# Turning the third batch's context behind the first residuals, and issuing the first x2's transposes ahead of the second half of w2

## The chip, the cores and the metric

The kernel runs on one core of one Trainium2 chip. The metric is the device time of one execution in microseconds (us), as the median of the runs. TensorE (PE) multiplies, VectorE (DVE), ScalarE (ACT) and GpSimd (POOL) do the rest, and SyncE (SP) issues nearly all DMAs from one queue of its own, in program order.

## The reference, cut to what matters

Four batches of 512 rows of width 512, with a context of 512 rows of width 256 each, go through cross attention and a feed-forward layer whose weights are quantised to -1, 0 and 1 inside the kernel.

```python
def _bit_quant(w):
    scale = jnp.maximum(jnp.mean(jnp.abs(w)), EPS)
    w_ternary = jnp.clip(jnp.round(w / scale), -1.0, 1.0)
    return w + jax.lax.stop_gradient(w_ternary - w)

# attention, teacher_logits = layernorm(x), teacher_features = ctx
query = einsum('bnc,dc->bnd', ctx, Wq) + bq
key = einsum('bnc,dc->bnd', ctx, Wk) + bk
attention = softmax(einsum('bnd,bmd->bnm', query, key), axis=-1)
x = x + einsum('bln,bmn->blm', layernorm(x), attention)

# feed-forward, w1 is (2048, 512), w2 is (512, 2048)
h = gelu(einsum('bsd,fd->bsf', layernorm(x), _bit_quant(w1)) + b1)
x = x + einsum('bsf,df->bsd', h, _bit_quant(w2)) + b2
```

The scale of a weight matrix is a mean over the whole matrix: nothing of w2 can be rounded before the last quarter of w2 has landed and been summed.

## The kernel before, in words

Each engine has a program written out by hand, and semaphores tie them together; an engine does its instructions in exactly the order written. Batches are numbered 0 to 3, and each has four row tiles of 128.

SP loads ctx 0, x 0, the biases, ctx 1, x 1, then w1 (two halves, each four DMAs of 512 KB, L253), ctx 2 (`load_ctx(2)`, L245), then both halves of w2 (`load_w(1, 0)` and `load_w(1, 1)`, L253 too). Then it issues `turn_x2(0)` (L257): two DMA transposes of the layer-normed x2 of batch 0, one for its high fp16 part and one for its low part, 512 KB each, from a staging area (`gT_lo` for batch 0) into `x2T`. SP waits for `x2_hi_done` ahead of the first and for `x2_lo_done` ahead of the second. Behind them stand b2, x 2, ctx 3 and x 3.

DVE turns a context by a 32x32 block transpose (`turn_ctx`, L735), which the projections (PE, L409) need. After the attention product of batch 0 (PE, L460) it adds the residual (`residual`, L794), takes the moments (`moments2`, L800, and `aggregate2`, L807), and POOL makes x2n of them (`layernorm2`, L325 to L350). ACT casts x2n to its high part (`high_x2`, L648) and DVE subtracts for the low part (`low_x2`, L755). DVE also copies the low part of the turned probabilities of batch 1 (`low_turned_probs(1)`, L741).

The scale of w1 and of w2 is found like this: ACT sums absolute values of eight chunks (`sum_abs`, L672; chunks 0 to 3 are the first half of the matrix in SBUF, 4 to 7 the second, and it waits for each half's semaphore), DVE adds the eight sums (`abs_rows`, L811), PE sums over the partitions (`total`, L441), and DVE makes the scale and its inverse (`quantiser_scale`, L815 and L818). POOL then rounds the matrix in eight chunks of two instructions (`round_weights`, L372 and L375), and DVE clamps and turns each chunk (`quantise`, L849 and L856).

PE's order around the change is: attend(0), the turned probabilities of batch 1 (L435), project(2) (L409), attend(1) with total(W1) inside it, the first quarter of the hidden layer of batch 0 (`hidden(0, 0)`, L475, 32 matmuls), total(W2), the other three quarters (96 matmuls), and the output product of batch 0 (`output(0, t)`, L492), which needs the turned chunks of w2 one after another. The hidden layer goes through four PSUM banks: ACT applies the gelu (L680), writes the high part (L685), DVE writes the low part (`low_gelus`, L862), and only then may PE write the bank again.

ACT's order is: `sum_abs(0, (6, 7))`, `copy_qk(2)` (L622, which copies the projections of batch 2 out of PSUM), `high_x2(0)`, `sum_abs(1, range(8))`, then the gelus of batch 0. DVE's order there is `low_x2(0)`, `residual(1, 0)`, `quantiser_scale(W1)`, the other residuals of batch 1 among quantise(0, 0..3), `abs_rows(W2)`, `low_gelus(0, (0, 1))`, `quantise(0, 4)`, `low_gelus(0, (2, 3))`, `quantiser_scale(W2)`.

Of the kernel before, what the change touches and what calls it, by code (L numbers as in the profile page):

```python
# [25 lines left out]
def xattn_ffn(nc, x, ctx_in, Wq, bq, Wk, bk, w1, b1, w2, b2, out):  # L26
# [20 lines left out]
    with ExitStack() as stack:  # L47
# [64 lines left out]
        def x2_stage(b):  # L112
            return lo_stage[:, 0] if b == 0 else w1_stage[:, b % 2]

        def xn_stage(b):
            return w2_stage[:, 0]

        def probs_stage(b):
            return w2_stage[:, 1]
# [14 lines left out]
        def xnT(b):  # L134
            return turned_half(b, 0)

        def probsT(b):
            return turned_half(b, 1)
# [88 lines left out]
        def e_rows(tile):  # L227
            return tile.rearrange("p (s i) -> p s i", s=2)
# [10 lines left out]
        @block.sync  # L239
        def _(sp):  # L240
            def load_ctx(b):
                if b:
                    sp.wait_ge(ctxT_ready, b)
                for q in range(Q):
                    sp.dma_start(ctx_sb[q * R:(q + 1) * R], ctx_view[b, q]).then_inc(ctx_here, 16)  # L245

            def load_x(b):
                sp.dma_start(x_sb[:, b], x_tiles[b]).then_inc(x_here[b], 16)

            def load_w(m, h):  # L250
                n = raws[m].shape[1] // 2
                for q in range(Q):
                    sp.dma_start(raws[m][q * R:(q + 1) * R, h * n:(h + 1) * n, :],  # L253
                                 w_views[m][q, :, h * n:(h + 1) * n, :]).then_inc(w_here[m][h], 16)

            def turn(dst, stage, v, here):
                sp.dma_start_transpose(dst[:, v].rearrange("p j (t k) -> p (j t) k", t=NT), stage[:, v]).then_inc(here, 16)  # L257

            def turn_x2(b):
                if b >= 2:  # L260
                    sp.wait_ge(hidden_ready, NF * (b - 1))
                sp.wait_ge(x2_hi_done, NT * (b + 1))
                turn(x2T[:, b % 2], x2_stage(b), 0, x2T_here[b])
                sp.wait_ge(x2_lo_done, NT * (b + 1))
                turn(x2T[:, b % 2], x2_stage(b), 1, x2T_here[b])

            def turn_xn(b):
                if b > EARLY:
                    sp.wait_ge(attn_ready, NT * b)
                sp.wait_ge(xn_hi_done, NT * (b - EARLY + 1))  # L270
                turn(xnT(b), xn_stage(b), 0, xnT_here[b - EARLY])
                sp.wait_ge(xn_lo_done, NT * (b - EARLY + 1))
                turn(xnT(b), xn_stage(b), 1, xnT_here[b - EARLY])

            def turn_probs(b):
                sp.wait_ge(probs_hi_done, NT * (b - EARLY + 1))
                turn(probsT(b), probs_stage(b), 0, probsT_here[b - EARLY])
                sp.wait_ge(probs_lo_done, NT * (b - EARLY + 1))
                turn(probsT(b), probs_stage(b), 1, probsT_here[b - EARLY])

            def store(b, tiles=range(NT)):
                for t in tiles:
                    sp.wait_ge(y_done, NT * b + t + 1)
                    sp.dma_start(out_tiles[b, :, t], x_sb[:, b, t]).then_inc(out_done, 16)

            load_ctx(0)
            load_x(0)
            sp.dma_start(bqk[:, 0:1], bq.rearrange("(p a) -> p a", a=1)).then_inc(bqk_here, 16)
            sp.dma_start(bqk[:, 1:2], bk.rearrange("(p a) -> p a", a=1)).then_inc(bqk_here, 16)
            load_ctx(1)  # L290
            load_x(1)
            load_w(0, 0)
            load_w(0, 1)
            load_ctx(2)
            load_w(1, 0)
            load_w(1, 1)
            turn_x2(0)
            sp.dma_start(b2_sb[:], b2.rearrange("(a d) -> a d", a=1).to_broadcast([P, D])).then_inc(b2_here, 16)
            load_x(2)
            load_ctx(3)  # L300
            load_x(3)
            turn_x2(1)
            turn_xn(2)
            turn_probs(2)
            store(0)
            turn_x2(2)
            turn_xn(3)
            turn_probs(3)
            store(1)
            turn_x2(3)  # L310
            store(2)
            store(LAST, range(NT - 1))
            for n, columns in enumerate(HALVES):
                sp.wait_ge(y_done, NT * B + n)
                sp.dma_start(e_rows(out_tiles[LAST, :, NT - 1])[:, :, HALF_ROWS[n]],
                             e_rows(x_sb[:, LAST, NT - 1])[:, :, HALF_ROWS[n]]).then_inc(out_done, 16)
            sp.wait_ge(out_done, 16 * (B * NT + 1))
# [412 lines left out]
        def _(dve):  # L730
            def turn_ctx(b):
                dve.wait_ge(ctx_here, 16 * Q * (b + 1))
                if b:
                    dve.wait_ge(qk_ready, 2 * b)
                nc.vector.transpose(ctxT[:].rearrange("p k (tb r) -> p tb k r", r=R),  # L735
                                    ctx_sb[:].rearrange("p tb (c k) -> p tb k c", c=R)).then_inc(ctxT_ready, 1)

            def low_turned_probs(b, tiles=range(NT)):
                for j in tiles:
                    dve.wait_ge(probsT_hi_done, NT * b + j + 1)  # L740
                    nc.vector.tensor_tensor(probsT(b)[:, 1, j], ps_t[j][:], probsT(b)[:, 0, j],  # L741
                                            ALU.subtract).then_inc(bank_read[j], 1)

            def low_turned_xn(b):
                for j in range(ND):
                    dve.wait_ge(xnT_hi_done, ND * b + j + 1)
                    nc.vector.tensor_tensor(xnT(b)[:, 1, j], ps_t[j][:], xnT(b)[:, 0, j],
                                            ALU.subtract).then_inc(bank_read[j], 1)
# [49 lines left out]
            def moments2(b, t):  # L798
                dve.wait_ge(x2_done, NT * b + t + 1)
                nc.vector.bn_stats(stats2[:, t], x_sb[:, b, t]).then_inc(stats2_done, 1)  # L800

            def aggregate2(b):
                if b:
                    dve.wait_ge(rstd2_done, b)
                for t in range(NT):
                    dve.wait_ge(stats2_done, NT * b + t + 1)
                    nc.vector.bn_aggr(mv2[:, t], stats2[:, t]).then_inc(mv2_done, 1)  # L807

            def abs_rows(m):
                dve.wait_ge(abs_done, NCH * m)  # L810
                nc.vector.tensor_reduce(abs_row[:, m:m + 1], abs_sum[:, m - 1], AX.X, ALU.add).then_inc(abs_row_done, 1)  # L811
# [87 lines left out]
            for t in range(1, NT):  # L899
                inverse(1, t)  # L900
            low_turned_xn(1)
            turn_ctx(2)
            for t in range(NT):
                residual(0, t)
                moments2(0, t)
            aggregate2(0)
            low_turned_probs(1)
            abs_rows(W1)
            low_x2(0)
# [137 lines left out]
```

## Time and profile before

| | us |
|---|---|
| median of 3 runs | 326.37 |
| lowest and highest | 325.68, 327.33 |
| the profiled execution: its own time | 325.16 |
| the profiled execution: its span in the trace | 323.6 |
| PE busy | 306.2 (95% of the span) |
| DVE, ACT, POOL busy | 167.8, 146.9, 114.4 |

The profile is of one execution, and starts of instructions are counted in us from its span's start. An entry such as "[7.05 <-DMA x2T<-gT_lo]" behind an instruction says how long its engine was idle ahead of it and what ended that. A row of the timeline can merge several instructions of one kind ("x32"). The mean granted clock of TensorE is 0.989 of full speed.

### The profile page before, as it was taken

What the parts mean: (1) busy time and instruction counts of PE and PEld (TensorE: products, weight loads), DVE (VectorE), ACT (ScalarE), POOL (GpSimd) and SP (SyncE); (2) the same over time, 40 slices, a digit from 0 to 9 for tenths busy, and PEclk for the clock granted to TensorE, in tenths of its full rate; (3) what the DMA queues carried; (4) which work ended last, traced back from release to release, by engine and by line L of the source; (5) the groups of instructions that cost most, each with busy time, mean ns of one, the idle gap of its engine ahead of it and who ended that gap; (6) DMA issues with size and microseconds to landing.
All of it is one profiled execution on the core that took longest, in us unless ns stands there. A gap on an engine that the chain in (4) does not pass through costs nothing.

```text
span 323.6 us, 3680 instructions
## 1 busy us (share of the span) xinstructions
PE 306.2 (95%) x1397; PEld 143.8 (44%) x1397; DVE 167.8 (52%) x295; ACT 146.9 (45%) x255; POOL 114.4 (35%) x124
## 2 busy tenths in 40 slices
PE   6989999199999799999999999999999999999995
PEld 3445454044444344444444444444444444444454
DVE  2896398847999587463533822533533103342101
ACT  2186977657750752564274350565260006772000
POOL 0355017998999976000280470000290000000000
PEclk9999999789999999999999999999999999999999
DMA  8999999992000497500003676000006210000011
GB/s 218 255 207 213 195 222 214 177 240 77 0 2 0 83 131 144 164 2 0 0 0 67 125 135 194 2 0 0 2 4 117 75 51 15 0 2 0 32 61 38
DMA packets 57857, 28.03 MB, mean 87 GB/s; under 512 B 42736, under 2 KB 51696, under 8 KB 57840
## 3 DMA queue, kind: packets, MB, share of 16 engines
q1 hardware_dynamic: 57472, 27.53, 40.4%
q10 hardware_dynamic: 368, 0.27, 0.4%
q8 instruction: 11, 0.18, 0.2%
q14 instruction: 6, 0.05, 0.1%
HBM read 15.21 MB, written 4.19 MB: 60 GB/s over the span
## 4 chain that ended last, share of the span: by engine, by line
PE 67%; POOL 11%; SPq 10%; DMA 5%; DVE 3%; ACT 1%; issue 1%; POOLq 0%
PE ps_t L475 28%; PE ps_e L492 28%; PE ps_e L460 6%; SPq L253 5%; DMA ctx_sb<-in_ctx 3%; POOL w_raw L372 3%; POOL w_raw L375 3%; SPq L245 3%; POOL x2n L350 2%; PE ps_e L499 2%; DMA x2T<-gT_lo 2%; PE ps_e L416 2%; SPq L257 2%; POOL x_sb L366 2%; PE ps_e L409 1%
## 5 line engine op out<-in xcount | busy, mean ns | idle before, releaser
L475 PE MATMUL ps_t<-x2T,w1T 128*128 128x512 f16 x512 | 113.7, 382 | 7.1 <-DMA x2T<-gT_lo 7.1
L492 PE MATMUL ps_e<-w_raw,gT_hi 128*128 128x512 f16 x240 | 91.0, 379 | 0.0
L492 PE MATMUL ps_e<-w_raw,gT_lo 128*128 128x512 f16 x240 | 91.0, 379 | 0.0
L680 ACT ACTIVATE ps_t<-ps_t,b_col 128x512 f32<-128x512 f32 x64 | 42.5, 665 | 94.8 <-PE ps_t L475 94.8
L475 PEld LDWEIGHTS ps_t<-x2T,w1T 128*128 128x128 f16 x512 | 50.4, 99 | 68.6 <-DMA x2T<-gT_lo 7.5
L862 DVE SCALAR_TENSOR_TENSOR gT_lo<-ps_t,h_scale,gT_hi 128x512 f16<-128x512 f32 x64 | 44.9, 743 | 64.8 <-ACT gT_hi L685 64.8
L685 ACT ACTIVATE gT_hi<-ps_t,h_scale 128x512 f16<-128x512 f32 x64 | 40.3, 685 | 0.0
L868 DVE SCALAR_TENSOR_TENSOR x_sb<-ps_e,h_unscale,x_sb 128x512 f32<-128x512 f32 x15 | 11.2, 747 | 55.2 <-PE ps_e L492 55.2
L325 POOL TENSOR_SCALAR var_eps<-mv 128x4 f32<-128x4 f32 x8 | 1.9, 240 | 98.7 <-DVE mv L807 86.1
L492 PEld LDWEIGHTS ps_e<-w_raw,gT_lo 128*128 128x128 f16 x240 | 23.5, 98 | 29.3 <-issue 1.7
L492 PEld LDWEIGHTS ps_e<-w_raw,gT_hi 128*128 128x128 f16 x240 | 23.5, 98 | 29.1 <-issue 1.2
L375 POOL TENSOR_SCALAR w_raw<-w_raw 128x1024 f16<-128x1024 f32 x16 | 21.8, 1363 | 1.4
L460 PE MATMUL ps_e<-w_raw 128*128 128x512 f16 x96 | 21.7, 379 | 0.0
L358 POOL TENSOR_SCALAR probs<-probs,row_inv 128x512 f32<-128x512 f32 x16 | 13.9, 885 | 21.3 <-DVE row_inv L780 21.3
L366 POOL TENSOR_TENSOR x_sb<-x_sb,b_sb 128x512 f32<-128x512 f32 x16 | 21.3, 1362 | 0.0
L372 POOL TENSOR_SCALAR w_raw<-w_raw,inv_scale 128x1024 f32<-128x1024 f32 x16 | 19.2, 1202 | 3.2 <-DVE inv_scale L818 3.2
L628 ACT ACTIVATE probs<-ps_e,row_max 128x512 f32<-128x512 f32 x16 | 10.9, 686 | 19.0 <-DVE row_max L775 18.9
L672 ACT ACTIVATE abs_out<-w_raw 128x1024 uint8<-128x1024 f32 x16 | 17.0, 1061 | 1.4 <-DMA w_raw<-in_L_ffn_w 1.0
L416 PE MATMUL ps_e<-qkT 128*128 128x512 f32 x32 | 14.9, 598 | 2.5 <-ACT probs L628 1.8
L409 PE MATMUL ps_e<-ctxT,WT 128*128 128x512 f32 x32 | 14.5, 595 | 1.4 <-DVE ctxT L735 1.4
L460 PEld LDWEIGHTS ps_e<-w_raw 128*128 128x128 f16 x96 | 9.4, 98 | 11.3
L350 POOL TENSOR_SCALAR x2n<-x_sb,neg_mean,rstd 128x512 f32<-128x512 f32 x16 | 14.0, 888 | 0.5
(82 smaller groups left out, 275.7 us busy)
## 6 DMA issues: line engine op xcount, KB each, us to landing
w_raw<-in_L_ffn_w SPq DMA_DIRECT2D x16, 512.0 KB, 10.4
x_sb<-in_x SPq DMA_DIRECT2D x4, 1024.0 KB, 6.8
out<-x_sb SPq DMA_DIRECT2D x15, 256.0 KB, 2.5
ctx_sb<-in_ctx SPq DMA_DIRECT2D x16, 128.0 KB, 5.1
b_sb<-in_L_ffn_b SPq DMA_DIRECT2D x1, 256.0 KB, 6.7
out<-x_sb SPq DMA_DIRECT2D x2, 128.0 KB, 2.2
x2n<-in_L_xattn_Wq ACTq DMA_DIRECT2D x1, 128.0 KB, 2.6
x2n<-in_L_xattn_Wk ACTq DMA_DIRECT2D x1, 128.0 KB, 3.3
```

What stands on the lines that cost most here:

```text
L350: nc.gpsimd.tensor_scalar(x2n[:, t].rearrange("p (j q c) -> p q j c", j=ND, q=Q), x_sb[:, b, t].rearrange("p (q j c) -> p q j c", q=Q, j=N ...
L366: nc.gpsimd.tensor_tensor(x_sb[:, b, t], x_sb[:, b, t], b2_sb[:], ALU.add).then_inc(b2_added, 1)
L372: nc.gpsimd.tensor_scalar(src, src, inv_scale[:, m:m + 1], ROUND, ALU.mult, ALU.add).then_inc(scaled, 1)
L375: nc.gpsimd.tensor_scalar(chunk_whole(m, c).rearrange("p n (i s) -> p n s i", s=2), src, -ROUND, 1.0, ALU.add, ALU.mult).then_inc(rounded, 1)
L409: mm = nc.tensor.matmul(ps_e[s][:], WT[:, s, k], ctxT[:, k], start=(k == 0), stop=(k == NC - 1))
L416: nc.tensor.matmul(attn_bank(b, t)[:], qkT[:, 0, t * P:(t + 1) * P], qkT[:, 1], start=True, stop=True).then_inc(scores_ready, 1)
L460: mm = nc.tensor.matmul(attn_bank(b, t)[:], xnT(b)[:, u, j, t * P:(t + 1) * P], probsT(b)[:, v, j], start=(n == 0 and j == 0), stop=(n == ...
L475: mm = nc.tensor.matmul(ps_t[t][:], w1T[:, k // 2, j, :, k % 2], x2T[:, b % 2, v, j], start=(v == 0 and j == 0), stop=(v == 1 and j == ND ...
L492: mm = nc.tensor.matmul(y_bank(t)[:], part[:, k, t * P:(t + 1) * P], w2T[:, k], start=(k == 0 and part is gT_hi), stop=(k == NF - 1 and pa ...
L680: nc.scalar.activation(ps_t[t][:], ps_t[t][:], ACT.Gelu, scale=1.0 / LN_SCALE, bias=b1_col[:, k:k + 1]).then_inc(gelu_done, 1)
L685: nc.scalar.activation(gT_hi[:, k], ps_t[t][:], ACT.Identity, scale=h_scale[:, 0:1]).then_inc(gT_hi_done, 1)
L862: nc.vector.scalar_tensor_tensor(out=gT_lo[:, k], in0=ps_t[t][:], scalar=h_scale[:, 0:1], in1=gT_hi[:, k], op0=ALU.mult, op1=ALU.subtract) ...
```

## The change

Two steps of two programs are written in another place; nothing is added or taken out. On SP, `turn_x2(0)` now stands between the two halves of w2. On DVE, `turn_ctx(2)` now stands behind the four residuals and the moments of batch 0, ahead of the low parts of the turned probabilities of batch 1.

```diff
             load_ctx(2)
             load_w(1, 0)
+            turn_x2(0)
             load_w(1, 1)
-            turn_x2(0)
             sp.dma_start(b2_sb[:], b2.rearrange("(a d) -> a d", a=1).to_broadcast([P, D])).then_inc(b2_here, 16)
...
             low_turned_xn(1)
-            turn_ctx(2)
             for t in range(NT):
                 residual(0, t)
                 moments2(0, t)
             aggregate2(0)
+            turn_ctx(2)
             low_turned_probs(1)
```

On SP the piece of the program between w1 and b2 reads as follows (L253 is a load of weights, L245 of ctx, L257 a transpose of x2's staging area, L298 b2):

```order
 L253 DMA w_raw<-in_L_ffn_w 32x32x128 x8
 L245 DMA ctx_sb<-in_ctx 32x16x64 x4
-L253 DMA w_raw<-in_L_ffn_w 32x8x512 x8
+L253 DMA w_raw<-in_L_ffn_w 32x8x512 x4
 L257 DMA_TRANSPOSE x2T<-gT_lo 128x16x128 x2
+L253 DMA w_raw<-in_L_ffn_w 32x8x512 x4
 L298 DMA b_sb<-in_L_ffn_b 128x512
 L248 DMA x_sb<-in_x 128x4x512
```

The last four loads of w2, and all behind them, now stand behind two instructions that wait for ACT and DVE.

On DVE, between the low parts of batch 1's turned xn (L747) and the first residual of batch 0 (L794), the context's turn is gone:

```order
 L747 TENSOR_TENSOR gT_hi<-ps_t2,gT_hi 128x512
 L747 TENSOR_TENSOR gT_hi<-ps_t3,gT_hi 128x512
-L735 STREAM_TRANSPOSE ctxT<-ctx_sb 128x16x2x32
 L794 SCALAR_TENSOR_TENSOR x_sb<-ps_e0,x_sb 128x512
 L800 BN_STATS stats2<-x_sb 128x6
```

The residuals of batch 0 no longer stand behind the wait for ctx 2. It comes back behind the eight instructions of residuals and moments and the aggregation, ahead of batch 1's turned probabilities (L741):

```order
 L800 BN_STATS stats2<-x_sb 128x6
 L807 BN_AGGR mv2<-stats2 128x2 x4
+L735 STREAM_TRANSPOSE ctxT<-ctx_sb 128x16x2x32
 L741 TENSOR_TENSOR gT_hi<-ps_t0,gT_hi 128x512
 L741 TENSOR_TENSOR gT_hi<-ps_t1,gT_hi 128x512
```

The projections of batch 2 (PE) and what copies them (ACT) wait for this instruction. PE, ACT and POOL keep their programs.

## Rows read from the trace of the kernel before

**Rows 1.** Waits of PE over the whole span: total us, times, longest

```profile
PE ps_t L475 <- DMA x2T<-gT_lo: 7.1, 1, 7.1
PE ps_e L416 <- ACT probs L628: 1.8, 1, 1.8
```

**Rows 2.** Chain that ended last, in order of time: start us, us, what

```profile
48.44 4.00 POOL x2n L350 x4
...
53.10 5.23 SPq L257
...
58.39 5.95 DMA x2T<-gT_lo
64.38 8.52 PE ps_t L475 x32
...
126.86 6.91 PE ps_t L475 x32
```

**Rows 3.** Timeline of DVE from 34 us: start us, us, instruction [idle before <-releaser]

```profile
39.82 1.25 DVE L735 STREAM_TRANSPOSE ctxT<-ctx_sb 128x1024 f32<-128x1024 f32 x1 [5.04 <-DMA ctx_sb<-in_ctx]
...
44.92 0.68 DVE L794 SCALAR_TENSOR_TENSOR x_sb<-ps_e,x_sb 128x512 f32<-128x512 f32 x1
...
49.89 3.92 DVE L755 TENSOR_TENSOR gT_lo<-x2n,gT_lo 128x512 f16<-128x512 f32 x4 [0.85 <-ACT gT_lo L648]
...
70.96 1.41 DVE L862 SCALAR_TENSOR_TENSOR gT_lo<-ps_t,h_scale,gT_hi 128x512 f16<-128x512 f32 x2 [3.92 <-ACT gT_hi L685]
```

**Rows 4.** Timeline of PE from 40 us

```profile
40.62 1.91 PE L435 MATMUL ps_t<-ident,probs 128*128 128x128 f32 x16
42.36 3.60 PE L409 MATMUL ps_e<-ctxT,WT 128*128 128x512 f32 x8
...
72.86 20.88 PE L475 MATMUL ps_t<-x2T,w1T 128*128 128x512 f16 x96
```

**Rows 5.** Timeline of ACT from 45 us

```profile
45.44 1.25 ACT L622 ACTIVATE qkT<-ps_e,bqk 128x512 f32<-128x512 f32 x2
...
58.64 1.06 ACT L672 ACTIVATE abs_out<-w_raw 128x1024 uint8<-128x1024 f32 x1 [0.97 <-DMA w_raw<-in_L_ffn_w]
...
63.15 0.19 ACT L672 ACTIVATION_READ_ACCUMULATOR abs_out<-w_raw 128x1 f32 x1
67.79 1.28 ACT L680 ACT_TABLE_LOAD   x1 [4.45 <-PE ps_t L475]
...
73.51 1.26 ACT L685 ACTIVATE gT_hi<-ps_t,h_scale 128x512 f16<-128x512 f32 x2
```

**Rows 6.** Timeline of SP's issues: start us, us on SP

```profile
37.56 0.45 SPq L253 DMA_DIRECT2D w_raw<-in_L_ffn_w  x1
...
108.88 1.89 SPq L257 DMA_TRANSPOSE x2T<-w_raw  x1
...
110.82 2.62 SPq L257 DMA_TRANSPOSE x2T<-w_raw  x1
```

**Rows 7.** DMA view, us from issue to landing: issue of 37.56, then of 110.82

```profile
w_raw<-in_L_ffn_w SPq DMA_DIRECT2D x1, 512.0 KB, 11.9
...
x2T<-w_raw SPq DMA_TRANSPOSE x1, 4.8
```

**Rows 8.** Windows: us, busy PE, PEld, DVE, ACT, POOL, PEclk, DMA share, GB/s

```profile
50.00:56.00 6.00, 6.00 (x29) 2.71 (x28) 5.60 (x10) 4.71 (x8) 3.58 (x4) 1.00 1.07 216
...
62.00:64.00 2.00, 0.00 (x0) 0.00 (x0) 1.93 (x4) 1.30 (x4) 1.91 (x3) 0.50 0.94 107
...
110.00:115.00 5.00, 3.91 (x14) 1.75 (x15) 2.77 (x5) 3.54 (x9) 4.89 (x6) 1.00 1.11 208
```

**Rows 9.** Timeline of POOL from 54 us

```profile
54.77 1.12 POOL L372 TENSOR_SCALAR w_raw<-w_raw,inv_scale 128x1024 f32<-128x1024 f32 x1 [2.34 <-DVE inv_scale L818]
...
73.77 1.34 POOL L375 TENSOR_SCALAR w_raw<-w_raw 128x1024 f16<-128x1024 f32 x1
75.99 1.25 POOL L372 TENSOR_SCALAR w_raw<-w_raw,inv_scale 128x1024 f32<-128x1024 f32 x1 [0.87 <-DVE inv_scale L818]
```

## The prediction, made before the changed kernel had run

> **What bounds the kernel now.** I read the waits of PE first: in the whole span PE waits long for one thing only, 7.1 us for the transposes of x2, and the next wait is 1.8 us for an exponential of batch 2 [rows 1]. PE is busy for 95% of the span (the table above), so only what lies before that second wait can move the end. The chain, read next, goes through exactly this place: POOL makes x2n until 52.44, ACT's last cast ends about 53.1, SP spends 5.23 us on the first transpose (its ring still holds w2), the second is issued at 58.39 and lands at 64.34, and PE starts the hidden layer at 64.38 [rows 2]. So the change attacks the longest wait of the kernel. But the chain does not stay with PE. POOL starts rounding w1 at 54.77, ends at 75.11, starts w2 at 75.99, for which it waited 0.87 us on the inverse scale [rows 9], and from there POOL, not PE, carries the chain through eight chunks of w2, b2, the second layernorm of batch 1 and the exponentials, to PE's wait of 1.8 us. In this stretch the end is therefore set by **when POOL may start w2**, and PE has 1.8 us of air. The question is what the change does to that start.
>
> **The context behind the residuals.** DVE sat idle for 5.04 us for ctx 2 while the attention products of batch 0 were coming out [rows 3]. PE ends the last of them at about 40.8 (it starts the next work at 40.62, with some overlap) [rows 4]. The first three residuals are then done, and the fourth starts at about 40.85 in place of 44.92 [rows 3], so POOL's x2n moves about 4.1 us forward, from 48.44 to 44.3, and ends at 48.3 [rows 2]. What it costs: the turn of the context, 1.25 us [rows 3], now starts when the aggregation is over, at 42.5, and ends at 43.7. PE's projection starts there and not at 42.36, takes its 3.60 us and ends at 47.3 [rows 4]. ACT copies the second of its two results only then, 0.6 us each [rows 5], to 47.9, and this stands ahead of the casts of x2n. Four casts at 0.65 us (the last ended 53.1, and four of them back to back take 2.6) end at 50.5: **2.6 us sooner, not 4.1**. DVE's four subtractions took 3.92 us [rows 3], start about 48.6 and end at 52.5, 1.3 us sooner than 53.8. DVE's scale of w1 comes right behind, so POOL starts w1 at about 53.5 instead of 54.77 and would end at 73.9 instead of 75.1 [rows 9].
>
> **The transposes ahead of half of w2.** The first half of w2 was issued by 37.56 and landed 11.9 us later, at 49.5 [rows 6, 7]. The ring is then empty. The nearest rows for a transpose pair from an empty ring are those of batch 1: issued at 108.88 and 110.82, SP held for 1.89 and 2.62 us, the second landing 4.8 us after its issue [rows 6, 7]. From 50.5 this gives the first issue at 50.5, the second at 52.5, landing at 57.3: 7 us sooner than 64.34. PE is in attend(1) until about 58.6 (57.3, which is 64.38 less its wait of 7.1, plus the 1.35 us by which the projection is late), so hidden(0, 0) starts there, 5.7 us sooner, with no idle time ahead of it, at the full clock, in 6.91 us, and ends at 65.5 [rows 2].
>
> **What stands behind the moved transposes.** SP issues the last four loads of w2 after them, at 52.5 + 2.6 = 55.1, in place of right behind the issue of 37.56. Before, DMA was full all the time: 216 GB/s and a share of 1.07 between 50 and 56 [rows 8], and the second half landed at 58.6, 9.1 us behind the first (ACT's wait ended by it) [rows 5, 7]. Now DMA lies idle from 49.5 to about 51.6, and then moves the 1 MB of the transposes first. The half is 2.10 MB: 9.7 us at 216 GB/s, 9.1 us by the landings; I take 9.4. It starts when the transposes are through: 57.3 + 9.4 = **66.7, which is 8 us later** than 58.6.
>
> Who waits for it: ACT. Its chunks 4 to 7 took from 58.64 to 63.34, 4.7 us [rows 5], and stand ahead of every gelu. They end at 71.4. Before, ACT was through at 63.34 and idle for 4.45 us until PE's first tiles; the table load started at 67.79 [rows 5]. Now it starts at 71.4, 3.6 us later, though PE has had the four tiles ready since 65.5. From here the steps are counted in rows of before: DVE's first low part started 3.17 us after the table load (70.96 against 67.79) [rows 3, 5], so with 1.41 us for the first two DVE is busy until 4.6. The second pair's high parts can start 4.7 us after the table load: 1.28 for it, 2.3 for the first pair's gelus and high parts, 1.16 for two gelus. The high parts' start to POOL's start on w2 was 73.51 to 75.99, 2.5 us [rows 5, 9]; about 0.25 us is added by quantise(0, 4), which stands between the pairs on DVE. Together 7.45 us: POOL starts w2 at 71.4 + 7.45 = 78.9, against 75.99 [rows 9]: **2.9 us later**. The 2.2 us that POOL's earlier end of w1 might have given become idle time of POOL.
>
> PE's own way: bank 0 is read 3.9 us after the table load, so hidden(0, 1) starts at 71.4 + 3.9 = 75.3, against 72.86 [rows 4], 2.4 us later. PE is idle for 9.8 us ahead of it. In its idle time of before the granted clock fell to 0.50, which is 1.2 GHz [rows 8], and the first 32 matmuls took 8.52 us where 32 take 6.91 at full clock [rows 2]: 1.6 us that are now paid behind this stall. PE would be 4.0 us late, and with its 1.8 us of air [rows 1] 2.2 us late. POOL is the later one. The loss is POOL's 2.9 us, since from PE's wait of 1.8 us on nothing is idle that could take it back.
>
> **The sum.** Against the profiled execution's own time, 325.16 + 2.9 = 328.1 (its span 323.6 becomes 326.5). That execution lay 1.2 us under the median of the runs, so against the median: 326.4 + 2.9 = 329.3.
>
> **A rule weighed.** Two transposes of 512 KB each kept DMA at a share of 1.11 and 208 GB/s between 110 and 115 [rows 8], 5 us for 1 MB. The Trainium skill, in "DMA: Bandwidth & Descriptors", section "Latency and other measured facts", gives 261 GB/s for such a transpose; an estimate by that page is 4.0 us for both, the half of w2 would land 1.0 us sooner, and the loss would be 1.9 us. The trace doesn't agree with it.
>
> **The rivals.** (a) *The half of w2 and the transposes overlap.* If it flows from its issue on, it lands at 55.1 + 9.4 = 64.5 and the loss is 0.7 us: 327.1, which is no change. Against it: batch 1's pair alone kept the DMA engines' share at 1.11 [rows 8], so it leaves no room for that. (b) *Faster.* The mechanism is that w2's scale is ready when POOL ends w1 at 73.9. Then POOL's chain is 1.2 us early and only that is gained, since POOL's rounding is the bound: about 325.2. It decides at a landing of 61.6 (73.9 less 7.45, less 4.7), 6.5 us after the issue at 55.1, with 1 MB of transposes ahead; the rows give more than 11. A change that gains more than 1.2 us I see no mechanism for. (c) *SP is held as it was before.* It spent 5.23 us on the first transpose in place of 1.89 [rows 2, 6]. If that was the transpose's own cost and not the full ring, the second is issued at 55.7 and everything behind it is 3.2 us later: a loss of 6.1, 332.5. (d) *PE becomes the bound* by a low clock that lasts. If the 32 matmuls of hidden(0, 1) ran wholly at 1.2 GHz, they cost 6.9 us and not 1.6: 2.4 + 6.9 - 1.8 = 7.5 us, 333.9. Rows of before show it for a part of the 32 only. In mild form (the half of w2 at 68, the same clock) it stays under POOL. (e) *The transposes start no sooner*, because ACT's casts don't move: then the pair is issued from 53.1 and the half of w2 is 2.6 us later still, 331.9. Against it: nothing else stands ahead of the casts.
>
> The Trainium skill, "TensorE: Matmul & The Clock Gate", section "HAM oscillation — how this bites in real kernels", says that a wait for DMA between bursts of matmuls puts the array back to its low clock each time. The trace agrees in the one wait it has (0.50 in rows 8); by this rule the new wait costs PE its start-up again, which is (d) in its mild form, and a kernel is not helped by trading one such wait for a longer one.
>
> **How the numbers follow.** The forecast, 2 to 5.2 us lost, has 0.68; a loss under that but above 1.6 us 0.05; (a), with what else lies within 0.5%, 0.14; (b) 0.02; (c), (d) and (e) together 0.09; 0.02 is left for a gain without a mechanism that I see. The range 326.8 to 331.6 takes in (a), and at its upper end the half of w2 at 9.7 us with 2 us more for a ring that starts from empty; it leaves out (b), (c), (d) and (e). A measurement of this kernel can tell about 0.5% (1.6 us) from no change. Faster by more than that 0.02, within it 0.16 ((a) and (b)), slower 0.82.
>
> **What would show it.** In the profile of the changed kernel: DVE's four residuals run before ctx 2 is turned, with the turn at about 42.5; the casts of x2n end about 50.5; the transposes are issued at 50.5 and 52.5; PE's 7.1 us wait at L475 for DMA is gone, and in its place hidden(0, 1) waits about 9.8 us for DVE's low parts of the gelus; ACT waits some 11 us at L672 for DMA of w2, until 66.7; POOL starts w2 at 78.9 after some 5 us of idle time. The prediction is wrong if ACT's wait ends before 65, or if POOL starts w2 before 77.6, or if PE's later wait at L416 doesn't stay (at 0.7 to 1.8 us), which would make PE the bound.

## The result, and the profile after

The changed kernel is slower, and by more than the range allowed for: 332.26 us (331.51 to 333.2) against 326.02 us (325.44 to 327.33), a ratio of 1.0187 with a 95% interval of 1.014 to 1.0234. That is 6.2 us where 2.9 were forecast. The profiled execution took 331.51 us with a span of 329.9 us. Three of the experiments below have one execution far out (939, 481 and 977 us), which is left out of their ratios and of the times given for them.

The waits of PE over the span, to hold against [rows 1]:

```profile
PE ps_e L441 <- DVE abs_row L811: 9.2, 1, 9.2
PE ps_t L475 <- DVE gT_lo L862: 3.2, 1, 3.2
...
PE ps_t L475 <- DMA x2T<-gT_lo: 0.3, 1, 0.3
```

The wait of 7.1 us for the transposes is down to 0.3, as meant. In its place PE waits 9.2 us for the sum of w2's rows and 3.2 us for the first gelus' low parts. The wait of 1.8 us at L416 is gone.

The first part of the change did what was expected of it. DVE's timeline, answering [rows 3]:

```profile
41.34 0.69 DVE L794 SCALAR_TENSOR_TENSOR x_sb<-ps_e,x_sb 128x512 f32<-128x512 f32 x1 [1.17 <-PE ps_e L460]
...
42.95 1.21 DVE L735 STREAM_TRANSPOSE ctxT<-ctx_sb 128x1024 f32<-128x1024 f32 x1
...
49.19 2.50 DVE L755 TENSOR_TENSOR gT_lo<-x2n,gT_lo 128x512 f16<-128x512 f32 x4 [2.59 <-ACT gT_lo L648]
```

The last residual starts at 41.34 and not at 44.92, the context is turned right behind the moments, and the low parts take 2.50 us in place of 3.92 and end at 51.7. The issues of SP and, from the DMA view, the times to landing of the transposes issued at 50.73 and 52.75 and of w2's loads issued at 56.47 and 58.07, answering [rows 6, 7]:

```profile
50.73 5.69 SPq L257 DMA_TRANSPOSE x2T<-gT_lo  x2
56.47 2.22 SPq L253 DMA_DIRECT2D w_raw<-in_L_ffn_w  x4
```

```profile
x2T<-gT_lo SPq DMA_TRANSPOSE x1, 6.4
...
x2T<-gT_lo SPq DMA_TRANSPOSE x1, 5.9
...
w_raw<-in_L_ffn_w SPq DMA_DIRECT2D x1, 512.0 KB, 6.1
...
w_raw<-in_L_ffn_w SPq DMA_DIRECT2D x1, 512.0 KB, 11.9
```

The second transpose lands at 52.75 + 5.9 = 58.65, 5.7 us sooner than before. The last quarter of w2 lands at 58.07 + 11.9 = 69.9, 11.3 us later than before. ACT, POOL and PE behind it, answering [rows 4, 5, 9]:

```profile
48.54 2.17 ACT L648 CAST gT_lo<-x2n 128x512 f16<-128x512 f32 x4
...
69.97 1.06 ACT L672 ACTIVATE abs_out<-w_raw 128x1024 uint8<-128x1024 f32 x1 [14.67 <-DMA w_raw<-in_L_ffn_w]
...
74.68 1.28 ACT L680 ACT_TABLE_LOAD   x1
```

```profile
52.65 1.12 POOL L372 TENSOR_SCALAR w_raw<-w_raw,inv_scale 128x1024 f32<-128x1024 f32 x1 [4.77 <-DVE inv_scale L818]
...
71.44 1.33 POOL L375 TENSOR_SCALAR w_raw<-w_raw 128x1024 f16<-128x1024 f32 x1
81.99 1.23 POOL L372 TENSOR_SCALAR w_raw<-w_raw,inv_scale 128x1024 f32<-128x1024 f32 x1 [9.22 <-DVE inv_scale L818]
```

```profile
58.73 7.08 PE L475 MATMUL ps_t<-x2T,w1T 128*128 128x512 f16 x32 [0.32 <-DMA x2T<-gT_lo]
75.00 0.56 PE L441 MATMUL ps_e<-abs_row,ones 128*128 128x1 f32 x2 [9.19 <-DVE abs_row L811]
...
78.75 22.83 PE L475 MATMUL ps_t<-x2T,w1T 128*128 128x512 f16 x96 [3.19 <-DVE gT_lo L862]
```

So PE does its first quarter early, at 58.73, and gains nothing from it: ACT is through with w2's sums at 74.66 (63.34 before), POOL ends w1 at 72.8 and starts w2 at 81.99, **6.0 us later** than at 75.99. PE's other three quarters start 5.9 us later and take 22.83 us in place of 20.88. The windows show why (columns as in [rows 8]):

```profile
68.00:70.00 2.00, 0.00 (x0) 0.00 (x0) 0.00 (x0) 0.03 (x1) 1.91 (x2) 0.74 1.05 300
70.00:72.00 2.00, 0.00 (x0) 0.00 (x0) 0.00 (x0) 1.97 (x3) 1.91 (x3) 0.50 1.05 371
...
80.00:82.00 2.00, 2.00 (x6) 0.71 (x5) 1.97 (x6) 0.71 (x2) 0.01 (x1) 0.50 0.00 0
82.00:84.00 2.00, 2.00 (x9) 0.87 (x8) 0.95 (x2) 0.66 (x1) 1.91 (x2) 0.85 0.00 0
```

The granted clock falls to 0.50 (1.2 GHz) after PE has stood still since 65.8, and is back between 82 and 84.

### The profile page after: what moved, and what is told of

Read it like the earlier page. It is cut to its first block, busy times and chain, and to the rows that moved or that the text cites. A ratio compares the mean times of both kernels' runs of the same rounds, so it can differ in the third digit from the quotient of the medians.

```text
span 329.9 us, 3680 instructions
## 1 busy us (share of the span) xinstructions
PE 307.9 (93%) x1397; PEld 144.6 (44%) x1397; DVE 165.4 (50%) x295; ACT 146.8 (44%) x255; POOL 113.3 (34%) x124
## 4 chain that ended last, share of the span: by engine, by line
PE 78%; DVE 7%; DMA 5%; ACT 4%; SPq 3%; issue 2%; DVEq 0%
PE ps_e L492 30%; PE ps_t L475 29%; PE ps_e L460 9%; PE ps_e L409 4%; DMA w_raw<-in_L_ffn_w 4%; PE ps_e L416 3%; PE ps_e L499 2%; DVE gT_lo L862 2%; SPq L257 2%; DVE tern L849 2%; DMA ctx_sb<-in_ctx 1%; ACT abs_out L672 1%; DVE ctxT L735 1%; ACT probs L628 1%; PE ps_t L435 1%
## 5 line engine op out<-in xcount | busy, mean ns | idle before, releaser
L862 DVE SCALAR_TENSOR_TENSOR gT_lo<-ps_t,h_scale,gT_hi 128x512 f16<-128x512 f32 x64 | 44.9, 743 | 65.4 <-ACT gT_hi L685 65.4
L868 DVE SCALAR_TENSOR_TENSOR x_sb<-ps_e,h_unscale,x_sb 128x512 f32<-128x512 f32 x15 | 11.2, 747 | 55.1 <-PE ps_e L492 55.1
L409 PE MATMUL ps_e<-ctxT,WT 128*128 128x512 f32 x32 | 16.0, 646 | 3.0 <-DVE ctxT L735 3.0
L416 PE MATMUL ps_e<-qkT 128*128 128x512 f32 x32 | 14.8, 595 | 0.7 <-ACT qkT L622 0.7
L460 PEld LDWEIGHTS ps_e<-w_raw 128*128 128x128 f16 x96 | 9.4, 98 | 11.3
L794 DVE SCALAR_TENSOR_TENSOR x_sb<-ps_e,x_sb 128x512 f32<-128x512 f32 x16 | 10.9, 680 | 4.4 <-PE ps_e L460 4.3
## 6 DMA issues: line engine op xcount, KB each, us to landing
w_raw<-in_L_ffn_w SPq DMA_DIRECT2D x16, 512.0 KB, 10.2
b_sb<-in_L_ffn_b SPq DMA_DIRECT2D x1, 256.0 KB, 11.9
```

The lines of the kernel that those rows point to most:

```text
L409: mm = nc.tensor.matmul(ps_e[s][:], WT[:, s, k], ctxT[:, k], start=(k == 0), stop=(k == NC - 1))
L416: nc.tensor.matmul(attn_bank(b, t)[:], qkT[:, 0, t * P:(t + 1) * P], qkT[:, 1], start=True, stop=True).then_inc(scores_ready, 1)
L460: mm = nc.tensor.matmul(attn_bank(b, t)[:], xnT(b)[:, u, j, t * P:(t + 1) * P], probsT(b)[:, v, j], start=(n == 0 and j == 0), stop=(n == ...
L862: nc.vector.scalar_tensor_tensor(out=gT_lo[:, k], in0=ps_t[t][:], scalar=h_scale[:, 0:1], in1=gT_hi[:, k], op0=ALU.mult, op1=ALU.subtract) ...
```

## The experiments

All ratios are to runs of the kernel before taken beside them on the same chip, with 95% intervals; those are what to compare, since the kernel before itself had medians of 326.2 to 327.3. Starts and spans are of one profiled execution each. They can lie over 1 us apart where nothing was changed: PE's projection (L409) starts at 42.36 in the kernel before [rows 4], and at 43.65 and 43.52 in two of the runs below (the transposes alone, and the kernel before with fillers) that leave all ahead of it as it was.

**Each part alone.** First the context's move by itself:

```diff
             low_turned_xn(1)
-            turn_ctx(2)
...
             aggregate2(0)
+            turn_ctx(2)
             low_turned_probs(1)
```

> Only the turn of ctx 2 is moved; the transposes stay behind all of w2. In the changed kernel's trace this move gave casts of x2n that ended at 50.7 in place of 53.1 and a start of w1's rounding at 52.65 in place of 54.77. Theory (the whole loss comes from the second half of w2 standing behind the transposes): here w2 lands at 58.6 as before, ACT's sums end at 63.3, and the transposes, issued into a full ring, land between 63.4 and 64.3; POOL starts w2 between 75.0 and 76.0. Time 325.0 to 326.4, that is 0 to 1.3 us under before. Rival (the move of the context costs by itself, since project(2), copy_qk(2) and attend(1) run 1.2 us later): 327 to 328.

Measured: 326.86 us, 1.0011 (0.998 to 1.0041), no change that can be told; the profiled execution took 326.56. SP and PE in its timeline:

```profile
52.13 10.21 SPq L257 DMA_TRANSPOSE x2T<-gT_lo  x2
...
64.39 9.89 PE L475 MATMUL ps_t<-x2T,w1T 128*128 128x512 f16 x32 [4.58 <-DMA x2T<-gT_lo]
```

The transposes are issued a microsecond sooner than before (52.13 against 53.10) and SP is then held for 10.21 us: they still go behind all of w2, and PE starts at 64.39, where it did before. The sooner moments end in the queue. The time can't tell the theory (0 to 1.3 us under before) from the rival (327 to 328, a ratio of about 1.002 to 1.005): the interval reaches into both. POOL's start on w2 between 75 and 76 was missed: it was 77.38, since hidden(0, 0) took 9.89 us; its granted clock was 0.50 until 70 us. Of the theory, the part that counts stands: without the transposes' move the loss is at most 0.4% (1.3 us), where it is 6.2 us with it.

Then the transposes' move by itself:

```diff
             load_w(1, 0)
+            turn_x2(0)
             load_w(1, 1)
-            turn_x2(0)
```

> Only the transposes are moved ahead of the second half of w2; the turn of ctx 2 stays where it was. Theory (every step from the casts to POOL's start on w2 is serial): the casts end at 53.1, 2.4 us later than in the changed kernel, so the last DMA of w2 lands at 72.3 instead of 69.9, POOL starts w2 at 84.4 instead of 82.0, and the time is 2.4 us over the changed kernel's 332.3: 334.7. Rival (the context's move is of no use where DMA, not DVE, sets the pace): 332.3, with the landing at about 70.

Measured: 334.14 us, 1.0259 (1.0217 to 1.0301), to be held against 1.0187 for both parts. ACT's and POOL's rows:

```profile
72.63 1.06 ACT L672 ACTIVATE abs_out<-w_raw 128x1024 uint8<-128x1024 f32 x1 [14.46 <-DMA w_raw<-in_L_ffn_w]
```

```profile
84.64 1.24 POOL L372 TENSOR_SCALAR w_raw<-w_raw,inv_scale 128x1024 f32<-128x1024 f32 x1 [9.26 <-DVE inv_scale L818]
```

w2 lands at 72.6 and POOL starts it at 84.64, within 0.3 us of what the theory gave. So the two parts are not independent: the context's move is worth nothing that can be told by itself and 2.7 us in POOL's start (84.64 against 81.99) once SP's queue stops for x2.

**How much stands behind the transposes.** Two of the four DMAs of the second half ahead of them, two behind:

```diff
-            turn_x2(0)
-            load_w(1, 1)
+            load_w2_part((0, 1))
+            turn_x2(0)
+            load_w2_part((2, 3))
```

> The changed kernel, but only two of the four DMAs of w2's second half stand behind the transposes, the other two ahead. Theory (the loss is the landing of the last DMA of w2, less ACT's idle time): two quarters less behind, 2.45 us each, the last lands at about 65.0 instead of 69.9, POOL starts w2 at 77.1, and the time is 4.9 us under the changed kernel's: 327.4, about 1.3 over before. Rival (the wait at the transposes itself is what costs, by stopping SP's queue, whatever the amount behind it): over 330.

Measured: 328.12 us, 1.0032 (1.0002 to 1.0062). ACT's wait ended at 65.4 and POOL started w2 at 77.41:

```profile
65.40 1.06 ACT L679 ACTIVATE abs_out<-w_raw 128x1024 uint8<-128x1024 f32 x1 [10.20 <-DMA w_raw<-in_L_ffn_w]
```

```profile
77.41 1.23 POOL L379 TENSOR_SCALAR w_raw<-w_raw,inv_scale 128x1024 f32<-128x1024 f32 x1 [4.95 <-DVE inv_scale L825]
```

The rival, that SP's stop costs whatever the amount behind it, falls: SP was held for 7.27 us at the transposes here too. The loss goes with the landing of the last quarter. Over the four kernels POOL's start is 1.4, 5.4, 6.0 and 8.7 us behind that of before (two behind, the run with the loads held, the changed kernel, the transposes alone), and the ratios give 1.0, 5.3, 6.1 and 8.4 us. The agreement is no better than 1 to 2 us: in the two runs with fillers in the changed kernel, further down, POOL starts w2 6.1 and 6.2 us late, and the ratios give 4.0 and 5.0 us.

**Why the half of w2 landed 3.2 us later than predicted.** Two runs take the term apart. In one, SP holds back b2, x 2, ctx 3 and x 3 until w2 has landed:

```diff
             turn_x2(0)
             load_w(1, 1)
+            sp.wait_ge(w_here[1][1], 16 * Q)
             sp.dma_start(b2_sb[:], b2.rearrange("(a d) -> a d", a=1).to_broadcast([P, D])).then_inc(b2_here, 16)
```

> The changed kernel, but SP waits for the second half of w2 to have landed before it issues b2, x 2, ctx 3 and x 3. In the changed kernel this half landed 11.3 us after the transposes (58.65 to 69.94), not 9.4 as predicted. Theory S (the loads issued right behind it share the DMA engines with it and slow it): here it lands at about 68.0, 9.4 us behind the transposes, and the time falls by about 1.9 us to 330.4. Theory R (it is the start of a run of loads behind the transposes that costs, whatever follows): it lands at 69.9 as in the changed kernel, and the time stays at 332.3, within 0.5 us.

Measured: 331.1 us, 1.0162 (1.0122 to 1.0202). ACT's wait for the last load:

```profile
69.37 1.06 ACT L673 ACTIVATE abs_out<-w_raw 128x1024 uint8<-128x1024 f32 x1 [14.13 <-DMA w_raw<-in_L_ffn_w]
```

It ends at 69.37, not 68.0. The first of the four loads is issued at 56.55, so the half takes 12.8 us from there; in the changed kernel it took 13.5. Theory R is the nearer one; what the loads behind cost is at most 0.7 us of the 3.2, in one profile each, and the times can't tell it from nothing. Counted from the transposes' landing, as the prediction counted, the half takes 10.6 us here (58.7 to 69.36) and 11.3 in the changed kernel, against 9.4. The windows of this run show that it isn't an idle start: from 57 to 67 the DMA share is 0.88 or more. But they give 57 GB/s from 68.0 to 68.5, 12 from there to 69.0 and then nothing, while the last load lands at 69.36: hardly anything moves in the last 1.4 us ahead of it. An interval between two landings of loads leaves such a stretch out.

In the other the half goes first, behind the wait for x2's low parts, from an empty ring (nothing of SP's queue is in flight), and the transposes behind it:

```diff
-            turn_x2(0)
+            sp.wait_ge(x2_lo_done, NT)
             load_w(1, 1)
+            turn_x2(0)
```

> The changed kernel, but SP waits for x2's low parts (about 51.7), then issues the second half of w2, and the two transposes behind it: the half starts from an empty ring with nothing ahead of it. It measures the term of 9.4 us by itself. If a start from an empty ring costs nothing beyond about 1 us, the half lands at 51.7 + 1 + 9.4 = 62.1. If the start costs as much as in the changed kernel (first quarter 6.1 us after its issue, then 2.45 us each: 13.5 us in all), it lands at 65.2. The transposes land about 5 us after it, so PE starts hidden(0, 0) at 67 to 70 with the clock down, and ACT's gelus start there; time 329 to 332.

The first load and then, from the DMA view, its time to landing:

```profile
52.34 0.31 SPq L253 DMA_DIRECT2D w_raw<-in_L_ffn_w  x1
```

```profile
w_raw<-in_L_ffn_w SPq DMA_DIRECT2D x1, 512.0 KB, 5.0
```

And where ACT's wait for the last one ends, with POOL's start on w2:

```profile
64.75 1.06 ACT L673 ACTIVATE abs_out<-w_raw 128x1024 uint8<-128x1024 f32 x1 [8.82 <-DMA w_raw<-in_L_ffn_w]
```

```profile
81.49 1.24 POOL L373 TENSOR_SCALAR w_raw<-w_raw,inv_scale 128x1024 f32<-128x1024 f32 x1 [8.13 <-DVE inv_scale L819]
```

The first quarter lands 5.0 us after its issue, the other three follow in 7.4 us. With nothing ahead of it, and the transposes behind it, the half takes **12.4 us from its first issue**, nearer to the 13.5 of the second expectation than to 10.4. Out of a full ring it added 9.1 us from landing to landing. A part of the 3.3 us between the two lies at both ends in this run's windows: no bytes move until 53.0, 0.7 us behind the issue, and from 64.0 to 64.5, just ahead of the last landing, they give 34 GB/s. In the full ring of the kernel before no microsecond from 41 to 56 has less than 207 GB/s. The time of this single execution was 330.62 us. POOL's start on w2 is late here for another reason than the landing: the transposes land last, PE starts hidden(0, 0) only at 68.95, behind a wait of 9.9 us, and the scale of w2 stands behind it.

**Which engine carries the lateness.** The changed kernel's L416 wait had gone, and by the prediction's own test that pointed to PE. Matmuls of no use keep the clock up, first in one of PE's two waits:

```diff
             hidden(0, 0)
             pe.wait_ge(x2_done, 2 * NT)
+            for _ in range(38):
+                nc.tensor.matmul(ps_e[2][:], w1T[:, 0, 0, :, 0], x2T[:, 0, 0, 0], start=True, stop=True)
             total(W2, ps_e[3])
```

> The changed kernel with 38 matmuls of 128x512 of no use (written to ps_e[2], whose content is not read) on PE behind hidden(0, 0), inside its wait of 9.2 us for w2's sums, so that TensorE's clock stays at 1.00. It separates PE's way from POOL's. Theory P (PE is the bound: hidden(0, 1..3) took 22.83 us instead of 20.88, and the output product followed): these 2 us come back but for the waits behind, 330.3 to 331.0, with hidden(0, 1..3) in 20.9 us. Theory Q (POOL's late start on w2 is the bound, as predicted): the time stays at 332.3, within 0.5 us, and PE waits about 2 us more for w2's chunks or for the exponentials.

Measured: 331.29 us, 1.0122 (1.0078 to 1.0167), a profiled span of 330.5 us, no shorter than the changed kernel's 329.9. The filler did not do its work: PE stood idle again behind the total, and the windows (columns as in [rows 8]) show the clock lost in the shorter of the two waits.

```profile
74.00:76.00 2.00, 0.65 (x4) 0.30 (x2) 0.16 (x1) 1.98 (x3) 0.00 (x0) 1.00 1.23 249
76.00:78.00 2.00, 0.00 (x0) 0.00 (x0) 0.05 (x1) 1.99 (x5) 0.00 (x0) 1.00 0.99 363
78.00:80.00 2.00, 1.16 (x3) 0.44 (x4) 1.97 (x4) 2.00 (x4) 0.00 (x0) 0.51 0.03 10
```

This run decides nothing. With 14 more behind the total it does:

```diff
             total(W2, ps_e[3])
+            for _ in range(14):
+                nc.tensor.matmul(ps_e[2][:], w1T[:, 0, 0, :, 0], x2T[:, 0, 0, 0], start=True, stop=True)
```

> The changed kernel with two fillers on PE: the 38 matmuls of no use of before the total of w2, and 14 more right behind it, in the wait of 3.4 us for DVE's low parts. With the first filler alone PE stood idle from 75.5 to 78.8, the granted clock was 0.51 from 78 to 80, and nothing came back, so P and Q were not told apart. Theory P (PE's way is the bound of the changed kernel): hidden(0, 1..3) now takes about 20.9 us instead of 22.8, and the time is 1.2 to 2.0 us under the changed kernel's. Theory Q (POOL's start on w2 is the bound): hidden(0, 1..3) is as much quicker, but the time stays within 0.5 us of the changed kernel's, and PE waits for w2's chunks or the exponentials instead.

Measured: 331.32 us, 1.0152 (1.0104 to 1.02), with a span of 329.8 us. PE's timeline, then its wait:

```profile
78.90 20.88 PE L475 MATMUL ps_t<-x2T,w1T 128*128 128x512 f16 x96 [0.35 <-DVE gT_lo L866]
```

```profile
PE ps_e L416 <- ACT probs L632: 1.9, 1, 1.9
```

The three quarters are 2 us quicker, at full clock, and the wait of 1.9 us for the exponentials is back: **the span doesn't move** (329.8 against 329.9). Theory Q holds by the traces. POOL starts w2 at 82.14 here, and the chain that ended last runs through POOL again: its late start on w2 is enough by itself to set the end, and the low clock only used up PE's air. In the changed kernel the chain runs through PE, so both ways end together there. The times alone can't tell P from Q: 1.0152 against 1.0187 is 1.1 us, and the intervals overlap.

**A version that gains.** POOL's start on w2 depended on the scale of w2, which waited for PE's first quarter and for gelus that it doesn't need. With the context's move, the transposes behind w2 as before, and the scale taken first:

```diff
+            pe.wait_ge(x2_done, 2 * NT)
+            total(W2, ps_e[3])
             hidden(0, 0)
-            pe.wait_ge(x2_done, 2 * NT)
-            total(W2, ps_e[3])
...
             abs_rows(W2)
+            quantiser_scale(W2)
...
             low_gelus(0, (2, 3))
-            quantiser_scale(W2)
```

> The turn of ctx 2 behind the residuals, the transposes behind all of w2, and the total and the scale of w2 made before hidden(0, 0) and not after it (PE: total(W2) ahead of hidden(0, 0); DVE: quantiser_scale(W2) right behind abs_rows(W2)). POOL then need not wait for PE's first quarter: it starts w2 when it ends w1, at 72.8 to 74.2 instead of 76.0. If POOL's chain is what PE's wait of 1.8 us at L416 waits for, this wait goes and the time is 1.0 to 1.8 us under before: 324.3 to 325.2. If the low clock in hidden(0, 0), 8.5 to 9.9 us for 32 matmuls, takes it back, 326.0 to 327.

Measured: 326.21 us, 0.9966 (0.9942 to 0.999), a small gain of 1.1 us by the ratio. That is the low end of the first expectation's 1.0 to 1.8; that the time itself lies in the second's 326 to 327 goes with the 327.3 us that the kernel before took beside it. The wait at L416 for the exponentials is gone and the chain runs through PE, as the first said, and the clock is low, as the second said. POOL no longer waits between w1 and w2, but PE starts 2.2 us later than before, at 66.55, because the total stands ahead of it and DVE makes the row sum only behind quantise(0, 3), and the clock is at 0.50.

> The kernel with the early total, and 20 matmuls of 128x512 of no use on PE (written to ps_e[2], not read) in the wait of about 5 us ahead of hidden(0, 0), so that the clock stays at 1.00. Theory (with POOL's chain early, PE is the bound from hidden(0, 0) on, and its low clock is paid in full): hidden(0, 0) takes 7.0 us instead of 8.5 to 9.9, and the time is 1.5 to 2.9 us under the kernel with the early total alone, 322 to 323.5. Rival (w1's chunks from POOL become the bound of the first quarter): hidden(0, 0) waits for DVE's turned chunks and the gain is under 0.5 us.

The filler is 20 matmuls ahead of the total:

```diff
+            pe.wait_ge(x2_done, NT + 3)
+            for _ in range(20):
+                nc.tensor.matmul(ps_e[2][:], gT_hi[:, 0, 0:P], gT_hi[:, 0], start=True, stop=True)
             pe.wait_ge(x2_done, 2 * NT)
             total(W2, ps_e[3])
             hidden(0, 0)
```

Measured: 325.09 us, 0.9929 (0.9898 to 0.9959). PE's four quarters, of this kernel with the filler and of the one without:

```profile
65.44 27.79 PE L475 MATMUL ps_t<-x2T,w1T 128*128 128x512 f16 x128
```

```profile
66.55 30.05 PE L475 MATMUL ps_t<-x2T,w1T 128*128 128x512 f16 x128
```

The 2.3 us are what the held clock gives; the median falls by 1.1 us, less than the 1.5 to 2.9 expected, with overlapping intervals, so that neither no gain nor the expected one is excluded. That the low clock counts here fits the chain of the kernel without the filler, which runs through PE's quarters and not through POOL. Then DVE's row sum and scale of w2 put ahead of quantise(0, 3):

```diff
             quantise(0, 2)
+            abs_rows(W2)
+            quantiser_scale(W2)
             aggregate2(1)
             quantise(0, 3)
-            abs_rows(W2)
-            quantiser_scale(W2)
```

> The kernel with the context's move, the early total and the filler, with DVE's sum of w2's rows and the scale of w2 ahead of quantise(0, 3), not behind it. There PE waited 2.4 us for that sum, until 65.2, though ACT's last chunk was done at about 64. Theory: PE starts hidden(0, 0) at the transposes' landing, about 64.3, and the time falls by 0.5 to 1.0 us. Rival (DVE, busy with low parts and w2's chunks from 80 to 100, is the bound by then): no change within 0.5 us.

Measured: 323.5 us, 0.9921 (0.9889 to 0.9953), so 3.0 us under the 326.5 us of before by the medians and 2.6 us by the ratio. PE starts hidden(0, 0) at 64.13, the wait of 2.4 us is down to 0.8. Against the kernel without this step nothing can be told (0.9921 against 0.9929; the spans are 321.4 and 321.3 us), which excludes neither the 0.5 to 1.0 us of the theory nor the rival's none. The rival named DVE; the trace names POOL. Its chain through eight chunks of w2 sets the end again, and PE waits 1.1 us for the exponentials at L416, for which it didn't wait in the kernel without this step:

```profile
PE ps_e L416 <- ACT probs L631: 1.1, 1, 1.1
```

Two runs ask which part of it is needed. The same kernel as the one with the filler, without the context's move:

> The kernel with the early total and the filler, but with the turn of ctx 2 where it was in the kernel before. It tells what the context's move is worth once POOL's chain is early and the clock is held. Theory (the moments 4 us sooner carry through to DVE's sums of w2, at 65.0 instead of 66.9, on which PE now waits): 1.5 to 2 us slower than with it. Rival (the move is worth nothing, as in the run with it alone, since w2's landing sets the pace): the same within 0.5 us.

Measured: 325.5 us, 0.9966 (0.9938 to 0.9994), against 0.9929 with it: the intervals overlap. The traces differ as the theory says, PE's hidden layer starting at 67.94 instead of 65.44, but also in the clock, since the filler had to wait for a residual until 60.45 and 32 matmuls ran partly low again. The worth of the context's move there stays open, between nothing and about 2.5 us.

And the kernel before with nothing but 24 fillers ahead of hidden(0, 0):

> The kernel before with 24 matmuls of no use in PE's wait of 7.1 us ahead of hidden(0, 0), nothing else. Theory: hidden(0, 0) takes 6.9 to 7.1 us instead of 8.5; POOL can start w2 only when it ends w1, 0.9 us sooner, and the wait of 1.8 us at L416 stays, so the time is 0.9 us under before, a ratio of 0.997. Rival (PE alone counts): 1.5 us under before or more, and the wait at L416 gets longer.

Measured: 325.9 us, 0.9986 (0.9958 to 1.0014), no change. PE and POOL:

```profile
65.73 7.07 PE L475 MATMUL ps_t<-x2T,w1T 128*128 128x512 f16 x32
```

```profile
75.90 1.24 POOL L372 TENSOR_SCALAR w_raw<-w_raw,inv_scale 128x1024 f32<-128x1024 f32 x1 [0.28 <-DVE inv_scale L821]
```

```profile
PE ps_e L416 <- ACT probs L631: 1.7, 1, 1.7
```

The clock is held and the quarter takes 7.07 us, but the filler itself was let go only at 60.54 by DVE's residual and ran on past the transposes' landing at about 64.1, so hidden(0, 0) starts 1.3 us late; POOL ends w1 at 75.6, half a microsecond later than before, and starts w2 where it did, and the wait at L416 stays. It agrees with POOL's chain as the bound of the kernel before; the gain of 0.9 us was not reached, nor excluded.

## Why the prediction was wrong

**Direction and mechanism: right.** It named the second half of w2 behind the moved transposes, ACT's sums in order ahead of the gelus, and POOL's start on w2 as what sets the end; PE's way came to the same length beside it, see below. Casts of x2n were to end at 50.5 (50.7 measured), PE to start at 58.6 (58.73), ACT's sums to take 4.7 us (4.69), and POOL to start w2 7.45 us after them (7.33). Two of these hits are partly luck. The casts start 0.6 us later than meant (48.54 for 47.9) and take 0.4 us less (2.17 for 2.6). PE was to be held by attend(1) until 58.6, with the transposes landed at 57.3; attend(1) ended at 58.41 and PE waited 0.32 us more, for the transposes. Other terms were off and cost nothing: DVE's subtractions took 2.50 us and not 3.92, so that POOL ended w1 at 72.8 and not 73.9, and was only idle longer. In rival (b) the landing that decides is 61.75 by its own terms (73.9 less 7.45, less 4.7), not 61.6.

**Size: the step that failed is the landing of the half of w2**, 66.7 predicted, 69.94 measured. All of the miss is there: 3.2 us late, and the loss is 3.3 us over the forecast's 2.9. It was worked out as 57.3 for the transposes plus 9.4 for the half, and both terms were short:

- The pair of transposes was to hold SP from 50.5 to 55.1. It held it from 50.73 to 56.42, and landed at 58.65: 1.35 us late. I took the pair of batch 1 as the nearest row. With the transposes alone moved, the pair took 6.8 us from its first issue to its landing; here, with the same two instructions, 7.9. The windows show where this 1.1 us lies: in the changed kernel the DMA engines move 2 and 9 GB/s from 55.5 to 56.0 and from 56.0 to 56.5, in the midst of the pair, where with the transposes alone moved no half microsecond from 55 to 60 has less than 164. What makes that gap is open.
- The half was priced by its share of a running stream, 9.1 us between two landings or 9.7 by the rate of a full ring. But such a run of loads takes 12.4 us from its first issue with nothing ahead, 12.8 behind the transposes, and 13.5 as it was; I had in effect allowed 11.6. Of the 1.9 us behind the transposes' landing (11.3 for 9.4) at most 0.7 is the loads right behind; what the windows show of the rest is that hardly anything moves in the last 1.4 us ahead of the landing in the run with the loads held, and it is not taken apart further. A margin of 2 us for the start stood in the range's upper end only, together with nothing for the transposes, and so the end of 331.6 was too low by 0.7. It belonged in the sum, and rows ahead of the prediction pointed to it: the pair of transposes of batch 1 took 6.7 us from the first issue to the last landing [rows 6, 7] where its bytes take 5 us at 208 GB/s [rows 8].

The upper end was also narrowed by hand: rival (c), SP held longer by the transposes, was real in part (1.1 of its 3.2 us) and had been left outside.

**PE or POOL.** The prediction gave PE 2.2 us and POOL 2.9, so that POOL decided. Both ways got the 3.2 us of the landing, PE lost 1.95 us to the clock and not 1.6, and 0.4 us to a chunk of w2, and they came out even: the L416 wait was gone. My test for "PE is the bound" (that wait gone) would have named PE alone; the run with the clock held shows that POOL by itself gives the same span. Whether PE's way by itself would do so too has no run. Rival (d) in its mild form happened and cost nothing that the span shows.

**Rivals.** (a), overlap of the half with the transposes, and (b), a gain, did not occur. (e) is excluded by the casts at 50.7; it is close to what the transposes' move gives without the context's, and there the loss was 8.4 us.

**The rule weighed.** The Trainium skill's 261 GB/s for a DMA transpose ("DMA: Bandwidth & Descriptors", "Latency and other measured facts") would have made the forecast worse. Here the pair took from 50.73 to 58.65, issue to landing, 1.2 us longer than the 6.7 us of batch 1 [rows 6, 7] and not shorter.

## What to carry to other kernels

When a transfer is moved ahead of another in one queue, price the one that now stands behind by a measured run of the same kind, issue of the first to landing of the last, and not by bytes over the rate of a full ring; here the wait at the head of the queue drained it. Then follow the later one to whoever must have all of it: a mean over a whole matrix makes its last quarter as urgent as the first. Where two engines' ways meet, a vanished wait doesn't tell which of them is the bound; take the cost off one and see whether the wait returns.

## What the runs showed of the hardware

- A run of four 512 KB loads from an empty ring: the first lands 5.0 us after its issue, the last 12.4 us after the first issue; in a full ring four such loads added 9.1 us. With nothing behind the four, the DMA engines moved 57 GB/s or less in the last 1.4 us ahead of the last landing.
- DMA transposes of 512 KB hold SP for 1.9 to 3.7 us each with no loads ahead of them in the ring, and both together for 10.2 us behind w2's loads (52.13 to 62.3).
- Behind 0.8 us of idle time, two tiny matmuls and 3.4 us more of idle time the granted clock was 0.51, the lower of its two levels (78 to 80 in the windows above). 32 matmuls of 128x512 took 6.91 to 7.08 us at the full clock, and 8.52, 9.44 and 9.89 us behind DMA waits of 7.1, 9.9 and 4.6 us. With the transposes alone moved a wait of 2.4 us was enough for 8.56 us, with two loads behind one of 1.9 us left the clock at 1.00 and they took 7.08: the length of the wait doesn't order the price.
- DVE's four subtractions for x2's low parts took 2.50 us where POOL stood idle beside them and 3.92 us where POOL was still making x2n (until 52.44 [rows 2]) and ACT's casts came one by one; how much of it is waiting for the casts and how much slower instructions was not taken apart.
